# A two-layer network on one core: the second layer routed and dispatched by sequences, and the attention's half groups in another order

## What is computed

```
xn = layernorm(x)
s  = causal attention(xn), 16 heads of 8, softmax, times WO
g  = silu(top-2 of 8 experts(xn), each silu(xn W1) * (xn W3), times W2)
x  = x + s * g
xn = layernorm(x)
s  = xn + MLP(layernorm(context(xn)))   # context: omega, cumsum, cos/sin, cumsum again
g  = silu(8 groups of 256 tokens, top-2 of 8 experts, at most 64 tokens
          for each expert in a group; gelu(x w0) * (x w1), times wo)
x  = x + s * g
```

## Time and profile before

| | us |
|---|---|
| median of three runs (lowest, highest) | 658.17 (657.75, 658.73) |
| the profiled execution | 658.66 |
| its span, first to last instruction | 656.9 |
| PE busy, share of the span | 594.7, 91% |
| DVE busy | 490.1, 75% |
| ACT busy | 325.3, 50% |
| POOL busy | 163.5, 25% |
| mean granted clock of PE | 0.964 of full speed |

### The profile page before, as it was taken

One profiled execution on the slowest core, in us unless ns is written; L12 is line 12 of the kernel. 1 busy time (PEld: TensorE's weight loads), 2 busy tenths in 40 slices (PEclk: granted clock), 3 DMA queues, 4 the chain that ended last, 5 costly groups with the idle time before them and its releaser, 6 DMA issues. The chain is left out here.

```text
span 656.9 us, 12382 instructions
## 1 busy us (share of the span) xinstructions
PE 594.7 (91%) x4214; PEld 365.6 (56%) x4215; DVE 490.1 (75%) x1169; ACT 325.3 (50%) x581; POOL 163.5 (25%) x146
## 2 busy tenths in 40 slices
PE   1878999999999999899999998949989799999996
PEld 0523644444453545899999843426446355555654
DVE  7799889999988898455555598246898288987455
ACT  1752367575766766555555467721323352254134
POOL 2000000000143441133333300000068668843200
PEclk9877799999999999999999999987999899999999
DMA  8980606060713181211111070061012114320232
GB/s 191 239 281 22 219 16 185 19 201 3 204 38 100 36 224 25 49 49 45 48 48 40 25 197 2 2 197 61 1 44 66 22 47 120 109 81 17 69 76 64
DMA packets 53692, 57.18 MB, mean 87 GB/s; under 512 B 8651, under 2 KB 37355, under 8 KB 53595
## 3 DMA queue, kind: packets, MB, share of 16 engines
q1 hardware_dynamic: 49310, 49.73, 27.1%
q0 software_dynamic: 4320, 6.81, 3.2%
q10 hardware_dynamic: 12, 0.01, 0.0%
HBM read 42.19 MB, written 18.85 MB: 93 GB/s over the span
## 5 line engine op out<-in xcount | busy, mean ns | idle before, releaser
L692 ACT ACTIVATE arena<-banks 128x512 f32<-128x512 f32 (+1 forms) x304 | 156.2, 586 | 100.3 <-PE banks L1588 57.9
L1602 PE MATMUL banks<-arena 96*128 96x512 bf16 (+3 forms) x384 | 120.4, 343 | 5.2 <-DVE mpart L1082 2.8
L1585 PE MATMUL banks<-arena 128*128 128x512 bf16 (+3 forms) x384 | 116.8, 331 | 6.5 <-ACT arena L692 2.8
L1085 DVE TENSOR_REDUCE mpart<-banks 128x1 f32<-128x512 f32 x128 | 85.8, 684 | 9.0 <-PE banks L1602 8.4
L1082 DVE CUSTOM_DVE_ANT_0 banks<-banks,arena 128x512 f32<-128x512 f32 (+1 forms) x128 | 78.9, 636 | 9.6 <-PE banks L1602 6.6
L1523 PE MATMUL banks<-arena 128*128 128x128 f32 x624 | 76.3, 275 | 1.0 <-ACT arena L642 1.0
L1523 PEld LDWEIGHTS banks<-arena 128*128 128x128 f32 x624 | 72.8, 192 | 1.5 <-ACT arena L642 1.5
L1644 PE MATMUL banks<-arena 128*9 128x512 f32 (+3 forms) x768 | 70.8, 487 | 0.0
L733 ACT ACTIVATE arena<-banks 125x512 f32<-125x512 f32 (+2 forms) x48 | 28.5, 595 | 81.0 <-PE banks L1757 57.0
L1585 PEld LDWEIGHTS banks<-arena 128*128 128x128 bf16 x384 | 38.0, 100 | 53.9 <-issue 26.0
L543 POOL DMA_INDIRECT slots<-rows_a,posn x16 | 15.5, 967 | 194.6 <-PE banks L1585 185.0
(11 more groups left out here) (289 smaller groups left out, 901.9 us busy)
## 6 DMA issues: line engine op xcount, KB each, us to landing
k_parts<-arena SPq DMA_DIRECT2D x6, 768.0 KB, 7.8
arena<-in_L_ffn_experts_w_dram SPq DMA_DIRECT2D x2, 2048.0 KB, 10.6
arena<-results SPq DMA_DIRECT2D x8, 512.0 KB, 6.8
arena<-k_parts SPq DMA_DIRECT2D x7, 576.0 KB
arena<-q_parts SPq DMA_DIRECT2D x28, 144.0 KB
arena<-in_L_ffn_w_kernel_dram SPq DMA_DIRECT2D x8, 344.0 KB
slots<-in_pad_rows_dram SPq DMA_DIRECT2D x1, 2535.0 KB, 11.0
arena<-slots SPq DMA_DIRECT2D x39, 65.0 KB
```

The lines of the kernel that those rows point to most:

```text
L692: act.activation(Pr[:, r % 4, heads[0]:heads[-1] + 1, 0:n], ring_e[e % 3][:, 0:len(heads) * n].rearrange("p (j c) -> p j c", j=len(heads)) ...
L1085: ins = dve.tensor_reduce(part, ps[:, 0:n], AX_X, ALU.max)
L1585: ins = pe.matmul(ring_e[e % 3][:, at * n:at * n + n], QK[:, slot, j, 1, P * kt:P * kt + P], QK[:, slot, j, 0, q:q + n], start=True, stop= ...
L1602: ins = pe.matmul(ps[:, at * n:at * n + n], QK[0:TALL, slot, j, 0, P * i:P * i + P], QK[0:TALL, slot, j, 1, 512 * half:512 * half + n], st ...
```

## The change

Two things are changed.

**Order of half groups.** `ORDER` lists half groups as (0, first), (1, first), (0, second), (1, second), and from group 2 on both halves of each group in turn. Exponentials, maxima, rows, products with V and turns follow it. The planner's ramp now ends after 22 exponential units instead of 11. SP stores the second sequence's parts before it loads group 1, follows `ORDER` with the rows of maxima, and loads group 3 after 49 units instead of 38.

```diff
+ORDER = [(g, 0) for g in range(2)] + [(g, 1) for g in range(2)] + [(g, h) for g in range(2, NG) for h in range(2)]
...
-    half0 = exp_units(QT // 2)
+    ramp = exp_units(SLOT[0, QT // 2])
...
             store_parts(0)
+            store_parts(1)
             load_group(1)
-            store_parts(1)
```

```diff
-          28: [("norm", 0)], 30: [("norm", 1)], 39: [("x_turn", 0)], 41: [("x_turn", 1)], 45: [("logits1",), ("scale",)]}
+          28: [("norm", 0)], 30: [("norm", 1)], 39: [("x_turn", 0)], 41: [("x_turn", 1)], 45: [("logits1",)], 46: [("route_max",)], 49: [("route_exp",), ("scale",)], 50: [("route_choice",)], 56: [("places1",)], 57: [("route_places",)]}
...
+            for g in range(3):
+                dispatch(g)
             for c in range(2, 4):
                 pe.wait_ge(Z["xn1_ready"], c + 1)
...
+            dispatch(3)
+            pe.wait_ge(Z["ld_L1"], 16 * 6)
+            for c in (1, 2, 0, 3):
...
-            for g in range(G1):
+            for g in range(G1 // 2, G1):
```

The slots and destinations on DVE, which before stood ahead of the experts, become steps of `recurrence`, and PE's `ones_d` product follows expert 0's down products:

```diff
+                if (e, k) == (0, 0):
+                    slot_of(0)
+                elif (e, k) == (1, 0):
+                    destination(0)
+                elif (e, k) == (2, 1):
+                    slot_of(1)
+                    destination(1)
...
+                    if (e, k) == (1, 1):
+                        pe.wait_ge(Z["wprep"], 1)
+                        for c in range(4):
+                            ins = pe.matmul(psO[:, 512:768], ones_d[:, :], W1g[:, c, :], start=(c == 0), stop=(c == 3))
+                        ins.then_inc(Z["wg_ps"], 1)
```

More of the change, by code:

```diff
@@ L87, in max_steps, with exp_units @@
     return steps
-def exp_units(stages):
-    return sum(len(exp_steps(r)) for r in range(stages))
-EXP_UNITS = exp_units(NS)
+def exp_units(slots):
+    return sum(len(exp_steps(*SLOTS[r])) for r in range(slots))
+EXP_UNITS = exp_units(len(SLOTS)) // NG
 TALL = 96
@@ L118, in count @@
             steps.append(due.pop(0)[1])
-    for g in range(NG):
-        for half in range(2):
-            for i in MAX_TILES[half]:
-                for step in max_steps(g, i):
-                    count(step)
-            steps.append(("negmax", g, half))
-            due.append([ROW_DELAY, ("maxrow", g, half)])
+    for g, half in ORDER:
+        for i in MAX_TILES[half]:
+            for step in max_steps(g, i):
+                count(step)
+        steps.append(("negmax", g, half))
+        due.append([ROW_DELAY, ("maxrow", g, half)])
     for d in due:
@@ L129, in maxima_stream, with routing_step @@
     return steps
-def routing_step(k, pair):
-    turn, rest = divmod(EXP_UNITS * (k - 1) + pair, 2)
-    if k < 1 or not rest:
+def routing_step(n):
+    turn, rest = divmod(n - EXP_UNITS, 2)
+    if turn < 0 or not rest:
         return []
@@ L192, in all_plans @@
-    return plans
-def value_steps(k, r):
-    if r % 2 == 0:
-        return []
-    if r == 1:
-        return [("pv", k - 1, NS - 2), ("pv", k - 1, NS - 1), ("evac", k - 1, 1)] if k > 0 else []
-    if k == NG:
-        return []
-    return [("pv", k, r - 3), ("pv", k, r - 2)] + ([("evac", k, 0)] if r - 2 == QT // 2 - 1 else [])
+    for r in range(len(SLOTS) + 3):
+        plan = plans.setdefault(r // NS, [])
+        exps = exp_steps(*SLOTS[r]) if r < len(SLOTS) else []
+        values = []
+        if r % 2 and r >= 3:
+            values = [("pv",) + SLOTS[r - 3], ("pv",) + SLOTS[r - 2]]
+            if r in evacs:
+                values.append(("evac",) + evacs[r])
+        for i, step in enumerate(exps):
+            plan.append(step)
+            n += 1
+            plan += maxima(OPENING + (LEAD + ramp - OPENING) * n // ramp if n < ramp else n + LEAD)
+            plan += routing_step(n - 1)
+            if since is not None:
+                since += 1
+                plan += MIDDLE.get(since, [])
+            if n % 4 == 0 and n <= 16:
+                plan.append(("logits", n // 4 - 1))
+            if i == (len(exps) - 1) // 2:
+                plan += values
+        if not exps:
+            plan += values
+        if r in turns:
+            plan.append(("turn",) + turns[r])
+        if r < len(SLOTS) and SLOTS[r] == EXPERTS_AT:
+            plan.append(("experts0",))
+            since = 0
@@ new lines, in route_places @@
+            def route_places(b, ps, read):
+                R, _, chosen = halves(b)
+                first, second, total = (ps[:, 64 * i:64 * i + 64].rearrange("p (n e) -> p n e", e=E) for i in range(3))
+                dve.wait_ge(Z["pre_ps"], 2 + b)
+                link(dve.tensor_scalar(R[7], total, float(C1), None, ALU.min))
+                dve.scalar_tensor_tensor(R[4], first, 1.0, chosen[0], ALU.add, ALU.mult)
+                dve.tensor_copy(R[5], first)
+                link(dve.tensor_tensor(R[6], second, R[7], ALU.add))
+                dve.sem_inc(read, 1)
+                link(dve.scalar_tensor_tensor(R[10], R[6], 1.0, R[3], ALU.add, ALU.mult))
+                link(dve.tensor_tensor(R[4], R[4], R[10], ALU.add))
@@ L1242, in _, with destination @@
                 link(dve.tensor_tensor(rows[a][:, :, W_META], r_[a], r_[5], ALU.mult))
-            for a in range(2):
+            def destination(a):
                 link(dve.tensor_tensor(r_[4], r_[6 + a], r_[2 + a], ALU.subtract))
@@ L1484, in _, with dispatch @@
+            def dispatch(g):
+                pe.wait_ge(Z["oh_ready"], g + 1)
+                ps, source = (banks[:, g, :], oh0) if g < G1 // 2 else (psM[:, g % 2, :], oh)
+                for i in range(2):
+                    ins = pe.matmul(ps, xn[:, 2 * g + i, :], source[:, (2 * g + i) % 8, :], start=(i == 0), stop=(i == 1))
+                ins.then_inc(Z["disp_ps"], 1)
             pe.wait_ge(Z["ld_spread"], 16)
```

262 lines of the change are left out of this document (134 added, 128 removed).

## The result

The changed kernel takes 665.91 us in the median of 4 runs (664.36 to 669.11), the kernel before 657.96 (657.33 to 658.73) beside it: a ratio of 1.0125, 95% interval 1.0090 to 1.0159. It is slower, by about 8 us, and lies above the range of the forecast (651.5 to 662.0). The profiled execution took 666.62 us with a span of 664.8.

The account below looks back on a forecast made before the run. Expert 4's start was taken as the bound: posn, 32 scatters, SP's read, weights. Posn -0.1 (+2.0 +1.0 -3.1) and scatters -4.6 gave -4.7; half clock +3.4 made -1.3, so 656.8 us, range 651.5 to 662.

Parts of the forecast that it names:

- expert 0 to the first scatter: Second layer: posn written 15.8 us after expert 0's first product, as slot and destination work moves into the experts.
- clock behind the idle stretch: At expert 4: after some 17 us idle, PE resumes at half speed for 6.8 us, costing +3.4 us (bounds 0 and 4.5).
- The opening: Kernel start: maxima spread evenly let DVE close its gaps, -3.1 us (bounds -5.0 and +2.0).
- I expect group 1 at about 46: Opening: group 1's load, queued behind a store, arrives before PE needs it at 47.13; up to 2 us late at worst.
- rival 2: Opening: group 1 lands late and the opening gives nothing, +3.1 us, end about 660; chance 0.12.
- The passage: From attention to second layer's experts: less routing and four fewer dispatches, so expert 0 begins at 463.0, 12.1 us earlier.
- rival 1: Passage: clock falls after a PE pause, omega is last, first late dispatch +3.5 us, end 660.3; chance 0.22.
- The price of 0.58 us for each microsecond of DVE's long operations: Second-layer experts: DVE's long SBUF operations lengthen POOL's scatters at this rate; 21.8 us of them cost 12.7.
- the -4.6: Second-layer scatters: 52.7 us instead of 57.3, since fewer long DVE operations run beside them.
- Rival 5: Scatters: every long vector operation stalls POOL for its whole length, 21.8 instead of 12.7, +9.1 us, 666; chance 0.03.
- into the same wait whether it stays or not: Between 511 and 528 us: an unexplained loss of about 8 us is absorbed by the wait before expert 4.
- PE idle 12 to 20 us before expert 4: Sign that the forecast is right: PE stands idle this long, then is released by the weight DMA.

Follow-up runs that it names:

- a_load_first: Changed kernel with SP again issuing group 1's loads ahead of the store of the second sequence's parts: 662.66 us, ratio 1.0099.
- o_shift_mm: a_order_old with 64 one-column products added on TensorE in the opening: 683.99 us.
- a_order_old: Changed kernel with the old order of half groups and group 1's loads first, leaving the second layer's part alone: 660.72 us, ratio 1.0044.
- o_again: a_order_old measured once more, unchanged, on another chip: 661.57 us, ratio 1.0046.
- o_shift: a_order_old with 128 empty instructions at the head of TensorE's program: 661.18 us.
- o_early: a_order_old with both destinations written earlier, behind the first products of experts 0 and 1: 654.51 us, ratio 0.9922.
- o_early_sp: o_early plus SP loading expert 4's weights before waiting for the scatters: 645.81 us, ratio 0.9785; measured again 652.17 us, 0.9902.

## Why the prediction was wrong

The prediction had expert 4 at 537.6 us; it began at 550.33, 12.7 us later. By its own steps:

| step | predicted | measured | miss |
|---|---|---|---|
| end of the attention (stream +1.0, opening -3.1) | 431.9 | 439.56 | +7.6 |
| from there to expert 0 | 29.0 | 33.7 | +4.8 |
| expert 0 to the first scatter | 18.2 | 17.9 | -0.3 |
| scatters, first start to last end | 52.7 | 53.4 | +0.6 |
| last scatter to SP to expert 4 | 5.9 | 5.8 | -0.1 |
| clock behind the idle stretch | +3.4 | 0 | -3.4 |

The misses add up to 9.2 us, and the medians are 9.1 apart (665.91 against 656.8).

**The opening** failed in its second part: "I expect group 1 at about 46". It was costed at -3.1 with a bound of +2.0, and measured +5.5; rival 2 had the mechanism, but priced it at 3.1 us over the forecast where the attention ended 7.6 over it. The working took the landing of the store's last part (45.4) as the load's arrival, added half a microsecond, and let the load's five issues end at 41.3. They ended at 44.15, and PE had what they brought 7.7 us after that. With the loads first (a_load_first) the q issues ended at 39.17, and at the same place PE went on at 44.63 without a wait. A load queued behind a store had to be costed as the store's end plus the load's own passage, and for that passage the working has no term. The gain of 3.1 us from a smoother DVE came at most by half: a_load_first, where nothing is late, has DVE busy 34.95 us in that stretch (34.37 in the earlier trace rows) and the attention ends only 0.4 us earlier than before. With the loads first it ends at 433.3 us in the mean of the three profiles with the new order (432.7 to 433.7) and at 434.9 in the mean of the ten with the old one and the same routing steps (433.6 to 436.8; o_shift_mm left aside).

**The passage** failed by rival 1, which had a chance of 0.22: behind the pause ahead of the turned rows (1.98 us) the clock fell to 0.50, from 447 on in a_order_old, and logits, dispatch 3 and a part of the omega products ran at half speed, so that PE and not the routing came last. The first remaining dispatch came 24.1 us behind the attention's end instead of 21.3, 2.9 us of the 4.8 (rival 1 had put them at 3.5). The other 1.9 us came behind it: the four dispatches took 8.83 us in the changed kernel (7.13 in a_order_old, 6.9 in the prediction), with the clock at 0.57 from 464 to 468. The prediction leaned on pauses of 1.7 us in the attention, where the clock stayed at 1.00. Why it fell here and not there these runs don't show.

**From expert 0 to expert 4** all totals held, to 0.6 us: the destinations' move into the recurrence costs 13.7 us (4.16 us behind expert 0 before, 17.89 after), shorter scatters give back 3.9 (51.3 against 55.2 from first start to last start), and SP and the weights are unchanged. For the scatters that total is partly luck. The price of 0.58 us for each microsecond of DVE's long operations is borne out: 9.3 us of lengthening beside 17.3 us of them here (0.54), and between 0.45 and 0.64 in all 17 profiles with such scatters. But the working expected 21.8 us of them, and they were fewer because DVE stood idle for the late signals (3.4 us less than costed). And it had no term for a scatter that must wait for a gated product of DVE, which here came late for the same reason:

```profile
530.57 1.31 DVE L1411 TENSOR_TENSOR arena<-banks,arena 125x512 f32<-125x512 f32 x2 [4.99 <-remote]
...
531.54 0.96 POOL L555 DMA_INDIRECT dest<-idt,posn  x1 [4.15 <-DVE arena L1411]
```

That is 3.85 us more than the 0.30 between scatters, and the two nearly cancel. Such a wait was there before too (2.75 us at 524.13), and the -4.6 set a measured 57.3 us against a sum that gives 54.1 for the kernel before. So the late signals act on the chain as well as on PE, in both directions.

Rival 5 named 666 us, which is the time measured, but by lengthening that didn't happen (0.54, not 1, for each microsecond): the agreement is chance. A slip without consequence: 463.0 - 2.1, 28 and 31 us make 519.9 for the end of expert 3, not 521.

That the 12 us won at the experts' start would be spent in a wait was right in kind. With the sizes as measured: +5.5 (opening), -7.3 (attention to expert 0), +13.7, -3.9, 0.0: +8.0 us at expert 4, which is the result.

**The late signals** were taken to go "into the same wait whether it stays or not". For the time it held, barely: in the changed kernel, a_order_old and o_again expert 4 still waited for its weights, for 1.26, 0.92 and 0.59 us, and in the profile of o_shift (11.2 us late, the slowest of its eight runs) it did not wait at all. But the sign "PE idle 12 to 20 us before expert 4" didn't show, for the late signals had eaten that idle time, and with it went the half clock behind it, which was priced at 3.4 and measured 2.4 us in o_early. That the stretch would grow from 4 to 14 us with the change, no step foresaw. And it matters as soon as the chain is mended: 6.4 us between the two measurements of o_early_sp's code.

**The larger miss is one of method.** The prediction saw that expert 4 waits for a chain that starts at posn, and that the change moves posn 14 us further behind expert 0, and still made the sum come out negative by two gains (3.1 us in the opening, 12.1 in the passage) that rested on nothing being late or slow there. By what was measured, the part behind expert 0 alone was +13.7 - 3.9 = +9.8 us, and the passage gave 7.3.

**A version that beats both.** The second layer's part with loads first, destinations written behind the first products of experts 0 and 1, and SP's read behind the load of expert 4: 0.9785 to 0.9902 of the time of before, 6 to 14 us less, depending on the late signals.

## What to carry to other kernels

When work is moved off a path to start a stage earlier, follow the item with the longest tail behind it (here 8 small vector operations, 32 scatters, a read, a weight load) and not the stage: a_order_old started the experts 8 us sooner and expert 4 3 us later, because the tail's first link moved 14 us further behind their start. A queue's order is priced by what is needed first: here stores ahead of a load cost 5.1 us, and no work behind took it up. And where two things end at the same time, both must be freed: freeing SP alone was worth nothing in the kernel before (1.0000), and beside earlier destinations it brought 0.9922 to 0.9785 on one chip.

## What the hardware did that was not expected

- What waited for TensorE's signals started 4 to 15 us late (DVE's copy 9.6 to 20.4 us after the start of products that take 5.5), from one place on, in 14 of 17 profiles with GpSimd's scatters 1.27 us apart: 3.9 to 6.2 us with 19 or 20 scatters started by then, 7.5 to 14.7 with 12. TensorE's products are in the trace at their full pace, so such a stretch looks like idle time with the releaser "remote" or "issue".
- Each microsecond of VectorE's long operations (128x1024 and 128x2048 elements, 1.23 or 2.29 us each) beside GpSimd's scatters lengthened these by 0.45 to 0.64 us in 17 profiles (14.1 us beside 24.3 before, 9.3 beside 17.3 after).
- Empty instructions on GpSimd (24 a scatter) and TensorE (128) changed no distance and moved no fetch against the program: 1.27 us still between scatters.
- One scatter of 128 rows of 4 bytes occupies GpSimd for 0.96 us, but the next, waiting for its landing, starts 2.87 us after it. The Trainium skill, "Perfetto Trace Analysis" (per-instruction lifecycle, SWDGE), says that the profiler's end of such an instruction is the end of descriptor generation and not of the data's movement; the rows agree, with 1.91 us between.
